# Latent parts ahead of the context scale, and their store and reload among the first transfers

## What is computed

```python
# cross attention: 16 heads of 64, keys and values from context and latents
xn = _layernorm(x, ln1_w, ln1_b)            # x: the context, 1024 rows a batch
ln = _layernorm(latents, ln2_w, ln2_b)      # latents: layernorm(x), 64 rows a batch
q = ln @ Wq
kv = jnp.concatenate([xn, ln], axis=-2) @ Wkv
k, v = jnp.split(kv, 2, axis=-1)
w = softmax(einsum('bhld,bhsd->bhls', q * scale, k * scale))
x = x + einsum('bhls,bhsd->bhld', w, v) @ Wo
# then x = x + mamba(layernorm(x)), a selective scan over 4 tiles of 128 tokens
# then x = x + moe(layernorm(x)), 8 experts with gelu, gathered and scattered by lists
```

## Time and profile before

| | before |
|---|---|
| runs (us) | 807.22, 808.18, 808.63 |
| profiled execution (us) | 806.97 |
| its span, first to last instruction (us) | 805.2 |
| mean granted TensorE clock | 0.966 |
| PE busy / PEld busy | 733.7 us (91%) / 675.1 us (84%) |
| DVE / ACT / POOL busy | 64% / 51% / 52% |
| bytes moved by DMA | 49.86 MB |

### The profile page before, as it was taken

How to read it: one execution, slowest core, us unless ns; L and a number is a source line. 1 busy time by engine, 2 the same in 40 slices (tenths; PEclk the granted TensorE clock), 3 DMA queues, 4 the chain that set the end, 5 groups by cost and what they waited for, 6 DMA issues and landing times.

```text
span 805.2 us, 14296 instructions
## 1 busy us (share of the span) xinstructions
PE 733.7 (91%) x5387; PEld 675.1 (84%) x5387; DVE 514.3 (64%) x1098; ACT 409.4 (51%) x1086; POOL 419.5 (52%) x373
## 2 busy tenths in 40 slices
PE   4949999999999999999899999999999768899996
PEld 3549999999999899999899899998999757448895
DVE  5326557557565677797958668887688769860102
ACT  2523544555344566555666466454766426634341
POOL 3904402701350179667836996587478889960000
PEclk9989999999999999999999999999999975899999
DMA  8461010011001100220012003100011114902710
GB/s 313 182 214 15 1 60 24 2 59 24 1 2 59 50 8 9 73 50 15 9 59 53 18 9 91 25 20 1 15 28 24 20 27 130 335 0 105 253 62 29
DMA packets 49481, 49.86 MB, mean 62 GB/s; under 512 B 18484, under 2 KB 44288, under 8 KB 48256
## 3 DMA queue, kind: packets, MB, share of 16 engines
q1 hardware_dynamic: 49408, 48.90, 19.6%
HBM read 44.10 MB, written 4.79 MB: 61 GB/s over the span
## 4 chain that ended last, share of the span: by engine, by line
PE 52%; POOL 20%; DVE 13%; issue 9%; ACT 3%; DMA 2%; SPq 1%; POOLq 0%; DVEq 0%; ACTq 0%
PE psum L1607 14%; PE psum L1640 13%; PE psum L1623 4%; POOL work L616 4%; POOL y_sum L629 4%; PE psum L2027 4%; POOL work L623 3%; PE psum L2017 3%; DVE work L930 2%; PE psum L1580 2%; PE psum L1697 1%; POOL ctx_nat L578 1%; PE psum L1669 1%; POOL ctx_nat L577 1%; POOL kvn_lo L592 1%
## 5 line engine op out<-in xcount | busy, mean ns | idle before, releaser
L1282 ACT ACTIVATE pt_hi<-psum 128x512 fp32r<-128x512 f32 (+1 forms) x192 | 87.1, 489 | 214.0 <-PE psum L1623 160.1
L1640 PE MATMUL psum<-kvn_hi,pt_hi 128*128 128x256 f32 x512 | 150.5, 294 | 0.8 <-DVE pt_hi L850 0.8
L1640 PE MATMUL psum<-kvn_hi,pt_lo 128*128 128x256 f32 x512 | 145.0, 283 | 0.0
L1640 PE MATMUL psum<-kvn_lo,pt_hi 128*128 128x256 f32 x512 | 144.8, 283 | 0.0
L993 DVE TENSOR_REDUCE rowmax<-psum 128x1 f32<-128x728 f32 x64 | 58.5, 914 | 74.4 <-PE psum L1607 74.1
L623 POOL TENSOR_TENSOR work<-work,bc 128x512 f32<-128x512 f32 x48 | 65.8, 1370 | 65.0 <-DVE work L930 65.0
L1640 PEld LDWEIGHTS psum<-kvn_hi,pt_hi 128*128 128x128 f32 x512 | 98.0, 191 | 1.1 <-DVE pt_hi L850 1.0
L1607 PE MATMUL psum<-kvt_hi,qk_hi 128*128 128x364 f32 (+1 forms) x384 | 91.7, 348 | 7.4 <-ACT prob L1405 4.2
L1640 PEld LDWEIGHTS psum<-kvn_lo,pt_hi 128*128 128x128 f32 x512 | 98.1, 192 | 0.1
L1640 PEld LDWEIGHTS psum<-kvn_hi,pt_lo 128*128 128x128 f32 x512 | 97.8, 191 | 0.0
L853 DVE TENSOR_TENSOR pt_lo<-psum,pt_hi 128x512 fp32r<-128x512 f32 x128 | 81.9, 681 | 8.7 <-ACT pt_hi L1282 8.7
(11 more groups left out here) (237 smaller groups left out, 1551.2 us busy)
## 6 DMA issues: line engine op xcount, KB each, us to landing
w<-in_L_ffn_W_dram SPq DMA_DIRECT2D x16, 1024.0 KB, 8.2
ctx_nat<-in_ctx_dram SPq DMA_DIRECT2D x8, 1024.0 KB, 5.0
bc<-dbc_keep SPq DMA_DIRECT2D x48, 128.0 KB, 4.5
q_keep<-q_t SPq DMA_DIRECT2D x1, 2048.0 KB, 8.4
q_cur<-q_keep SPq DMA_DIRECT2D x14, 128.0 KB, 3.1
wk_nat<-in_L_xattn_Wkv_dram SPq DMA_DIRECT2D x1, 1024.0 KB, 6.0
wq_sb<-in_L_xattn_Wq_dram SPq DMA_DIRECT2D x1, 1024.0 KB, 12.0
wv<-in_L_xattn_Wkv_dram SPq DMA_DIRECT2D x1, 1024.0 KB, 14.1
```

The source lines that it names most:

```text
L1282: act.activation(pt_hi[u][:, t0:t1, :], where[:, 0:(t1 - t0) * P].rearrange("p (t m) -> p t m", m=P), ACT.Copy)\
L1640: pe.matmul(PV, w[u][:, j, :], x_[slot][:, j, :], start=(j == 0 and w is pt_hi and x_ is kvn_hi), stop=False)
```

## The change

Two blocks move. On POOL, latent_parts() is called ahead of ctx_norm(0) instead of behind ctx_low(0, 0). On SP, the wait for s_xhl and the two stores to x_keep come ahead of latt_hi's store; the wait for st_x and the six loads of `load_latents` come right behind latt_hi's store, ahead of the wait for s_plo, latt_lo's store and q_keep's. No instruction is added or removed.

```diff
--- before.py
+++ after.py
@@ -404,18 +404,18 @@
                     rows = slice(h * DH, (h + 1) * DH)
                     sp.dma_start(q_cur[rows, :, h, :], q_keep[rows, :, b * L:(b + 1) * L]).then_inc(ld_q, 16)
 
+            sp.wait_ge(s_xhl, 2)
+            sp.dma_start(x_keep[:, 0], x_hi[:].bitcast(F32)).then_inc(st_x, 16)
+            sp.dma_start(x_keep[:, 1], x_lo[:].bitcast(F32)).then_inc(st_x, 16)
             sp.wait_ge(s_pevac, 2)
             sp.dma_start(latt_keep[:, 0], latt_hi[:].bitcast(F32)).then_inc(st_keep, 16)
+            sp.wait_ge(st_x, 32)
+            for b in range(2):
+                load_latents(b)
             sp.wait_ge(s_plo, 1)
             sp.dma_start(latt_keep[:, 1], latt_lo[:].bitcast(F32)).then_inc(st_keep, 16)
             sp.wait_ge(s_pqe, HP)
             sp.dma_start(q_keep, q_t[:]).then_inc(st_keep, 16)
-            sp.wait_ge(s_xhl, 2)
-            sp.dma_start(x_keep[:, 0], x_hi[:].bitcast(F32)).then_inc(st_x, 16)
-            sp.dma_start(x_keep[:, 1], x_lo[:].bitcast(F32)).then_inc(st_x, 16)
-            sp.wait_ge(st_x, 32)
-            for b in range(2):
-                load_latents(b)
 
             def load_weights():
 
@@ -661,12 +661,12 @@
                 pool.wait_ge(v_zc, t + 1)
                 pool.tensor_tensor(zs[t % 2][:], y_sum[:], zs[t % 2][:], ALU.mult).then_inc(v_y, 1)
 
+            latent_parts()
             ctx_norm(0)
             for q in range(4):
                 ctx_affine(0, q)
             ctx_high(0, 0)
             ctx_low(0, 0)
-            latent_parts()
 
             pool.wait_ge(s_misc, MISC)
```

## The result

The changed kernel took 802.88 us (median of 7 runs, 802.43 to 805.26); beside it the kernel before took 808.18 us (7 runs, 807.10 to 810.29). The ratio is 0.9941, 95% interval 0.9926 to 0.9957: **0.6% faster, 4.8 us by the ratio** (808.18 x 0.0059; the medians are 5.3 us apart), where 7.5 us had been forecast. In a second session the same kernel took 802.18 us against 808.21 (0.9928, 0.9911 to 0.9944), 5.8 us by the ratio.

A forecast was written before the change was run, and what follows sets the result against it. PE, busy 91% of the span, was held at the loop's start by batch 1's late context load through DVE's order. 5.50 + 2.05 = 7.55 us off 808.18 gives 800.6, stated as 800.7; range 798.6 to 803.4.

The forecast's parts named there:

- What held the loop up: Start of attention loop: batch 1's late context load holds DVE's statistics, hence the second row maximum and PE; 11.6 us attacked.
- The step of 5.50 us: Attention loop: PE's logits of head pair 2 start at 54.71 instead of 60.21, 5.50 us earlier.
- POOL's 0.25 us and its cover: Prologue: moved POOL work delays context work 0.2 to 0.3 us, hidden by PE's query projection with 1.0 us to spare.
- SP's queue: Prologue transfers: x_lo lands at 26, latt_lo's store slips to about 30, q_keep's undelayed, batch 1's context issued at 38.95.
- rival 4: SP caught at st_x: x_lo landing after 40.2 delays the context load; at worst about 811 us; chance 0.03.
- The clock's 2.05 us: Head pair 2's logits: shorter idle keeps the clock up, so they take 2.99 us instead of 5.04; lower bound 0.
- Rival 1: Head pair 2's logits: clock falls after the shortened idle too, only 5.50 to 6.8 us gained, 802.7 to 801.4; chance 0.24.
- Rival 2: Late stage from 630 us: one slow clock spell more or less, worth 2.05 us, 798.6 or 802.7; chance 0.10.

The follow-up runs named there:

- e2: Kernel before, with only batch 1's context load issued on SP ahead of the wait for the latents' parts, POOL untouched: 803.29 us, ratio 0.9937.
- e3: Kernel before, with only DVE's order changed: both halves of batch 1's statistics behind head pair 1's row maximum: 801.00 us, ratio 0.9915.
- e1: Kernel before with only POOL's part of the change (latent_parts() ahead of ctx_norm(0)), SP's order as before: 805.48 us, ratio 0.9967.
- e7: Changed kernel with idle transposes filling head pairs 0 and 1's idle stretches, plus 16, 20 and 12 in the prologue: 797.55 us, ratio 0.9863.
- e4: Changed kernel with 28 + 12 + 5 idle transposes on PE in the idle stretches of head pairs 0 and 1: 799.69 us, ratio 0.9893.

## Why the prediction was right and where it was wrong

**What held the loop up**: right. Moving the context load (e2), moving the wait on DVE (e3), or moving part of the way (e1, 3.0 us of load for 3.0 us of logits) each gave what the chain through DVE's order promised: e1 in its trace as well, e2 and e3 by their medians.

**The step of 5.50 us**: right. The third logits were to start at 54.71. They did at 54.57 and 54.74 in the two traces with a projection of 15.7 to 15.9 us, and at 55.37 where it took 16.47. The mean step over two traces and three is 5.4 us.

**POOL's 0.25 us and its cover**: 0.38 us by the affine's end, hidden as said. **SP's queue**: x_lo landed at 25.8 (17.11 + 8.7), 26 was said; the latents' loads, latt_lo at 29.62, q_keep unmoved by SP and the context at 39.14 (38.95) all came as written. The store's wait was far from the 40.2 us from which rival 4 would have counted.

**The clock's 2.05 us**: this is the term that was mis-sized, and the step of the prediction that failed. It measured 1.2 us: over three traces the third logits took 4.80, 3.27 and 4.60 us, a mean of 4.2, against 5.04 and 5.81 before, a mean of 5.4. Two things were wrong in it. First, the forecast judged the clock by the length of the idle time. That doesn't decide it alone: the same 1.42 + 0.81 us was followed by fast logits in one execution and by slow ones in another. Second, 2.99 us was the wrong length even for fast logits, since it was read where no wait stands ahead of them. With a wait ahead they take 3.23 to 3.28: the earlier trace rows has it in the first logits (39.69 to 42.92), and the changed kernel's second trace in the third (3.27). At full clock the term was thus worth at most 1.8 us. Rival 1, at 0.24, happened in two traces of three. Its text had the sentence that should have weighed more: the point at which the clock changes varies between executions, as the Trainium skill says ("TensorE: Matmul & The Clock Gate", Part 1). These traces now show it.

**A term that was missing: everything ahead of the loop held equal.** The sum took the one trace's projection, 15.63 us, for a fixed number. Five executions of the two kernels gave 15.63 to 16.73, each with a slow first part (e7 without one: 13.97). In two of them the granted clock fell in the wait for the query weights; in the other three no fall is recorded, but the transposes ahead of that wait were slow already. In the changed kernel's first trace it fell during 14 to 15 us (windows of 1 us: PE, PEld, DVE, ACT, POOL busy, clock, DMA share, GB/s):

```profile
14.00:15.00 1.00, 0.00 (x0) 0.00 (x0) 1.00 (x5) 1.00 (x2) 1.00 (x1) 0.88 1.04 422
...
21.00:22.00 1.00, 1.00 (x3) 0.52 (x2) 1.00 (x3) 0.00 (x0) 0.33 (x1) 0.71 1.12 400
```

This made that execution's projection 0.84 us longer than in the trace before. The forecast took over a short one by luck, and the kernel after the change feels the difference in full, while in the kernel before the load hid it (60.21 and 60.31).

**Rival 2, the late stage**: also real, and it went against the gain. The change's lead can be read off the same two instructions of ACT, an o_t of the attention and the first f_hi of the expert stage; first before, then the changed kernel's second trace:

```profile
602.90 0.28 ACT L1304 ACTIVATE o_t<-psum 128x128 f32<-128x128 f32 x1 [0.66 <-PE psum L1669]
```

```profile
713.86 0.40 ACT L1523 ACTIVATE f_hi<-dec 128x256 fp32r<-128x256 f32 x1
```

```profile
595.53 0.28 ACT L1304 ACTIVATE o_t<-psum 128x128 f32<-128x128 f32 x1 [0.66 <-PE psum L1669]
```

```profile
707.88 0.40 ACT L1523 ACTIVATE f_hi<-dec 128x256 fp32r<-128x256 f32 x1
```

602.90 - 595.53 = 7.37 us of lead, which is the forecast's 7.5, had become 713.86 - 707.88 = 5.98. Most of it went at one spot, where the clock fell between 606 and 611 in this execution and not in the first one before:

```profile
606.00:607.00 1.00, 1.00 (x33) 1.00 (x34) 0.97 (x2) 1.00 (x5) 0.97 (x1) 0.94 0.08 16
...
610.00:611.00 1.00, 1.00 (x7) 1.00 (x6) 0.00 (x0) 0.00 (x0) 0.92 (x2) 0.85 0.13 38
```

The kernel before has such a spell too in its second trace, from 615 to 620 (its lag against its first grows from 0.92 to 2.46 us there, and is 1.48 at f_hi). In the changed kernel's first trace 4.92 us of lead at the same two instructions became 4.48, in its third 5.99 became 5.31. So the late stage gives no systematic loss that I can prove: against the first trace before, the changed kernel loses 0.4 to 1.4 us there, and the kernel before itself loses 0.6.

Together, in means of two traces before and three after: a lead of 5.4 us at the start of the third logits, 6.6 at the fourth, 6.6 at that o_t, 6.0 at f_hi and 5.6 at the end; the two sessions gave 4.8 and 5.8. Of the forecast's 7.55 us, 0.1 is missing from the step, 0.8 from the clock's term, and 1.0 is lost behind the fourth logits, most of it after 600 us. This last part is rival 2's place; that it belongs to the change is not shown. The forecast of 7.5 is what one execution got up to 600 us, and none got at the end.

## What to carry to other kernels

When an engine's in-order list holds a wait for a prefetch ahead of work that the bounding engine needs, move that instruction or the prefetch's issue; the price is readable as one chain, and it held here to 0.2 us in two traces of three, to 0.7 in the third. Ask also what the late prefetch had been hiding: once it is gone, the variation of the engine ahead of it counts. Don't book what a fast clock would give from one execution's spell: count the clock's spells in two or three executions first, since they moved by more than 1 us per place, or fill the idle stretches nearly wholly, which here was worth 2.5 us in the loop (e4, with most of the spread) and about 5 with the prologue's (e7, another session). An instruction moved into an idle stretch of an engine is free only as long as the cover ahead of it is slow, and speeding the cover up brings it back.

## What was not expected of the hardware

The same matmul stream stood idle for the same 1.42 + 0.81 us in two executions of one program, and its next 18 matmuls took 3.27 and 4.60 us. A fill of 48 transposes in the prologue brought the projection from 15.6 to 17.0 us (eleven executions of all kernels here) down to 13.97, though the profile gives a granted clock of 1.00 for all of it in the trace before. Ahead of the first fall that it records, that row seems to read 1.00 whatever the clock was (the latents' eight transposes took 1.97 us in that trace and 1.10 in the one after, under the same row of 1.00). In six of those eleven these transposes took 1.97 us and no fall is recorded up to the projection's end; in the other five they took 1.09 or 1.10 us and a fall to 0.50 is recorded between 14 and 16 us. So the six fit a clock that was low from the start, but no row shows it directly.
